# Graph layer with x in halves: the degrees of strips 3 to 9 taken in two steps of 256 rows

## The reference

```
A     = adj + I
deg   = sum(A, axis=1)
d     = rsqrt(deg)
h     = ((A * d[:, None]) * d[None, :]) @ x
y     = x + elu(h @ w)
out   = (y - mean(y)) / sqrt(var(y) + 1e-5)
```

## Time and profile before

| | |
|---|---|
| median of 3 runs | 1055.69 us (1055.21 to 1061.57) |
| profiled execution | 1055.05 us, its span 1053.3 us |
| PE, weight loads | 923.3 us, 831.4 us busy |
| DVE, ACT, POOL | 763.8, 703.6, 194.3 us busy |
| read from memory | 360.78 MB, 16 DMA engines nearly always busy until 1000 us |
| mean granted TensorE clock | 0.968 of full speed |

### The profile page before, as it was taken

How to read it: one execution, slowest core, us unless ns; L and a number is a source line. 1 busy time by engine, 2 the same in 40 slices (tenths; PEclk the granted TensorE clock), 3 DMA queues, 4 the chain that set the end, 5 groups by cost and what they waited for, 6 DMA issues and landing times. The chain is left out here.

```text
span 1053.3 us, 35548 instructions
## 1 busy us (share of the span) xinstructions
PE 923.3 (88%) x16000; PEld 831.4 (79%) x16000; DVE 763.8 (73%) x633; ACT 703.6 (67%) x1677; POOL 194.3 (18%) x267
## 2 busy tenths in 40 slices
PE   0089399399797998999999999999999999999995
PEld 0065288287797898899998997999999999999994
DVE  0496497576587667868788767997988797866933
ACT  6898798898888898898989989862214715031201
POOL 0120120210401304040412433466001101000000
PEclk9999689799899899999999999999999999999998
DMA  9999999999999999999999999989998898899920
GB/s 385 401 387 413 399 393 402 396 400 396 399 394 387 379 387 393 336 391 392 392 395 394 385 396 389 357 272 311 376 304 277 284 326 290 303 304 309 352 80 21
DMA packets 168809, 367.28 MB, mean 349 GB/s; under 512 B 6224, under 2 KB 32976, under 8 KB 158416
## 3 DMA queue, kind: packets, MB, share of 16 engines
q1 hardware_dynamic: 151616, 356.54, 91.4%
q10 hardware_dynamic: 17040, 8.46, 2.8%
HBM read 360.78 MB, written 4.19 MB: 347 GB/s over the span
## 5 line engine op out<-in xcount | busy, mean ns | idle before, releaser
L892 PE MATMUL p_set<-space 32*128 32x256 f32 (+3 forms) x15872 | 906.9, 386 | 117.6 <-ACT space L800 56.1
L892 PEld LDWEIGHTS p_set<-space 32*128 32x128 f32 x15872 | 816.0, 188 | 204.1 <-issue 132.3
L910 DVE STREAM_TRANSPOSE space<-space 128x2048 f32<-128x2048 f32 x256 | 579.5, 2292 | 113.6 <-ACT space L792 86.2
L792 ACT ACTIVATE space<-space 128x512 f32<-128x512 f32 (+2 forms) x744 | 578.8, 779 | 83.4 <-DMA space<-in_adj 76.4
L934 DVE TENSOR_TENSOR hT<-p_set,hT 128x1024 f32<-128x1024 f32 (+2 forms) x109 | 105.9, 991 | 118.6 <-PE p_set L892 118.6
L792 ACT ACTIVATION_READ_ACCUMULATOR space<-space 128x1 f32 x744 | 138.8, 187 | 0.0
L815 ACT ACTIVATE space<-space 128x512 f32<-128x512 f32 x16 | 10.1, 631 | 181.5 <-DVE space L945 181.3
L775 POOL COPY space<-xn 32x512 f32<-32x512 f32 x192 | 120.0, 625 | 12.3
L759 POOL TENSOR_TENSOR d<-deg,half 128x4 f32<-128x4 f32 x16 | 16.3, 1017 | 541.7 <-DVE deg L916 541.7
L800 ACT ACTIVATE space<-xn 32x512 f32<-32x512 f32 x96 | 60.2, 627 | 47.8 <-POOL xn L765 38.9
L782 POOL TENSOR_TENSOR rstd<-var_eps,half 128x4 f32<-128x4 f32 x16 | 16.5, 1031 | 239.0 <-DVE var_eps L979 239.0
(11 more groups left out here) (16 smaller groups left out, 28.8 us busy)
## 6 DMA issues: line engine op xcount, KB each, us to landing
space<-in_adj SPq DMA_DIRECT2D x332, 1024.0 KB, 12.2
xn<-in_x SPq DMA_DIRECT2D x20, 256.0 KB, 11.2
space<-in_x ACTq DMA_DIRECT2D x16, 256.0 KB, 7.2
out_rows<-space ACTq DMA_DIRECT2D x16, 256.0 KB, 7.1
space<-in_adj SPq DMA_DIRECT2D x4, 768.0 KB, 12.3
ident<-in_w ACTq DMA_DIRECT2D x1, 64.0 KB, 5.3
```

The source lines that it names most:

```text
L792: ins = nc.scalar.activation(view[:, g], view[:, g], ACT.Copy, accum_out=to[:, g:g + 1])
L892: ins = nc.tensor.matmul(to, xs_chunk(h, j)[quadrant(q)], moving, start=first and s == b == 0, stop=last and s == b == 3)
L910: nc.vector.transpose(slots[slot], slots[slot]).then_inc(tile_turned, 1)
```

## The change

For strips 3 to 9 the degrees are found in two halves of 256 rows (blocks 0 and 1, then 2 and 3). The upper rows of all near tiles land first, then x is asked for (behind the first of the lower pieces), then the lower rows follow in one go. Each half has its own row sum, power, scaling and its own 16 copies, half as long. When the upper half of x is in place, PE may open up to two jobs (`HALF_JOBS`) of two or more tiles of that band that are already turned, and multiply them with the upper half (b = 0, 1); each keeps its PSUM set until the lower half follows. A single near tile is now loaded by two DMAs of 512 KB instead of one of 1 MB.

With it go other constants: `KEPT` loses 57 - 56 = 1 tile in all (band 8 keeps one more, band 10 two fewer, band 12 two more, band 15 two fewer), so that 80 tiles instead of 79 are loaded again, and `FEED` falls from 14 to 10. Bands 0 to 7 keep what they kept. The near tiles of strips 3 to 9 become 4, 5, 4, 4, 3, 4 and 3. The number of tiles to multiply stays 256. POOL's constant `half` is renamed `minus_half`.

```diff
-KEPT = (1, 2, 3, 4, 5, 6, 5, 4, 4, 4, 5, 4, 1, 2, 3, 4)
+KEPT = (1, 2, 3, 4, 5, 6, 5, 4, 5, 4, 3, 4, 3, 2, 3, 2)
...
+HALVED = range(3, 10)
+HALF_JOBS = 2
+PIECES = 2
...
-FEED = 14
+FEED = 10
...
+def halves_of(r):
+
+    return tuple(range(PIECES)) if r in HALVED else (None,)
...
-    return items + sorted((("near", t, r) for t in range(r, BANDS) if (t, r) in kept), reverse=True)
+    near = sorted((("near", t, r) for t in range(r, BANDS) if (t, r) in kept), reverse=True)
+    if r not in HALVED:
+        return items + near
+    return items + near + [("split", r), ("rest", r)]
...
-            base, t0, nk = runs[0], left[w - 1][1], BLOCKS // w
+            base, t0 = runs[0], left[w - 1][1]
+            nk = BLOCKS // max(w, len(halves_of(r)))
             group = len(groups)
-            groups.append([w, list(range(len(tiles), len(tiles) + w))])
+            some = []
+            groups.append([BLOCKS // nk, list(range(len(tiles), len(tiles) + w)), some])
             for i in range(w):
                 row_todo.remove(("near", t0 + i, r))
                 take_slot(("tile", len(tiles)), base + i)
-                tiles.append(("first", t0 + i, r, base + i, [len(loads) + j for j in range(w)]))
-            return [("near", r, nk * j, nk, t0, w, base, j, group) for j in range(w)]
+                tiles.append(("first", t0 + i, r, base + i, some))
+            return first_piece([("near", r, nk * j, nk, t0, w, base, j, group) for j in range(BLOCKS // nk)])
         _, t, r = row_todo.pop(0)
-        return [tile_load("first", t, r)]
+        if r not in HALVED:
+            return [tile_load("first", t, r)]
+        slot, some, group = take_slot(("tile", len(tiles))), [], len(groups)
+        nk = BLOCKS // PIECES
+        groups.append([PIECES, [len(tiles)], some])
+        tiles.append(("first", t, r, slot, some))
+        return first_piece([("near", r, nk * j, nk, t, 1, slot, j, group) for j in range(PIECES)])
+
+    def first_piece(these):
+
+        if these[0][1] not in HALVED:
+            return these
+        many = BLOCKS // PIECES
+        rest.extend(v for v in these if v[2] >= many)
+        return [v for v in these if v[2] < many]
...
+        if row_todo and row_todo[0][0] == "split":
+            row_todo.pop(0)
+            pending_x.append(at_row)
+        if row_todo and row_todo[0][0] == "rest":
+            row_todo.pop(0)
+            queued.extend(sorted(rest, key=lambda v: v[2] // (BLOCKS // PIECES)))
+            rest.clear()
+            if queued:
+                return queued.pop(0)
+            end_row()
...
+        if at_row not in HALVED:
+            pending_x.append(at_row)
...
+    def row_summed(load):
+
+        r = load[3] if load[0] == "tile" else load[1]
+        k0, nk = (0, BLOCKS) if load[0] == "tile" else load[2:4]
+        for half in halves_of(r):
+            many = BLOCKS if half is None else BLOCKS // PIECES
+            base = many * half if half is not None else 0
+            rows = len(set(range(k0, k0 + nk)) & set(range(base, base + many)))
+            wide = 1 if load[0] == "tile" else load[5] if load[0] == "near" else load[5] // BAND
+            if rows:
+                sums_left[r, half] -= rows * wide
+                if not sums_left[r, half]:
+                    offer("dve", 0, "row_sum", (r, half), 0.35)
...
+                took = 0.14 + {"dve": 0.52, "act": 0.52, "pool": 0.58}[e] / len(halves_of_home(h))
+                offer(e, 0 if some is FIRST_COPIES else 4, "copies", (h, half, i), took * len(pairs))
...
+        for n, (job, home, these, piece) in enumerate(half_jobs):
+            if piece in usable[home]:
+                half_jobs[n] = (job, home, these, piece + 1)
+                if piece == PIECES - 1:
+                    half_jobs.pop(n)
+                parts.append((job, home, these, False, piece == PIECES - 1, piece))
+                return len(parts) - 1
...
+            for t in HALVED:
+                if len(half_jobs) >= HALF_JOBS or t not in home_of or 0 not in usable.get(home_of[t], ()) or whole(t):
+                    continue
+                some = [i for i in turned_early if tiles[i][:2] == ("first", t)]
+                these = next((c for m in range(min(MERGE, len(some)), 1, -1) for c in map(in_steps, combinations(some[:8], m)) if c), [])
+                if these:
+                    for i in these:
+                        turned_early.remove(i)
+                    rows = [tiles[i][2] for i in these]
+                    job = open_job(rows, {u: 1 for u in rows})
+                    half_jobs.append((job, home_of[t], these, 1))
+                    parts.append((job, home_of[t], these, True, False, 0))
+                    return len(parts) - 1
...
+        def xs_part(h, half, q, s):
+
+            return slots[homes[h][1]][quadrant(q), blocks_of(half), F * s:F * (s + 1)]
+
+        def x_part(h, half, s):
+            return xn[quadrant(s), h % XN, blocks_of(half)]
...
-                    r = arg
-                    pool.wait_ge(row_summed, row_nth[r])
-                    nc.gpsimd.tensor_tensor(d[:, r], deg[:, r % 2], half[:, :], ALU.pow).then_inc(d_ready, 1)
+                    r, half = arg
+                    blocks = blocks_of(half)
+                    pool.wait_ge(row_summed, row_nth[arg])
+                    nc.gpsimd.tensor_tensor(d[:, r, blocks], deg[:, r % 2, blocks], minus_half[:, blocks], ALU.pow).then_inc(d_ready, 1)
...
-                    h = arg
-                    t = homes[h][0]
-                    pool.wait_ge(d_ready, power_nth[t])
+                    h, half = arg
+                    t, blocks = homes[h][0], blocks_of(half)
+                    many = blocks.stop - blocks.start
+                    pool.wait_ge(d_ready, power_nth[t, half] if first_home(h) else known_nth(t))
                     pool.wait_ge(x_loaded[h % XN], 16 * (h // XN + 1))
-                    nc.gpsimd.tensor_tensor(xn[:, h % XN], xn[:, h % XN], d[:, t].unsqueeze(2).to_broadcast([128, BLOCKS, F]), ALU.mult)\
-                      .then_inc(x_scaled, 1)
+                    nc.gpsimd.tensor_tensor(xn[:, h % XN, blocks], xn[:, h % XN, blocks],
+                                            d[:, t, blocks].unsqueeze(2).to_broadcast([128, many, F]), ALU.mult).then_inc(x_scaled, 1)
                 elif kind == "copies":
-                    h, some = arg
...
+                    h, half, some = arg
+                    earlier = [k for k, _ in order["pool"][:order["pool"].index((kind, arg))]]
+                    pool.wait_ge(x_scaled, earlier.count("scale"))
+                    pool.wait_ge(d_ready, earlier.count("power"))
+                    if "diagonal" in earlier:
+                        pool.wait_ge(diagonal_added, earlier.count("diagonal"))
                     wait_vacant(pool, ("home", h))
                     for s, q in copies_of(h)[some][1]:
-                        nc.gpsimd.tensor_copy(xs_part(h, q, s), xn[quadrant(s), h % XN]).then_inc(copied_by["pool"], 1)
-                        pool.wait_ge(copied_by["pool"], copied[h, (s, q)][1])
+                        nc.gpsimd.tensor_copy(xs_part(h, half, q, s), x_part(h, half, s)).then_inc(copied_by["pool"], 1)
...
-                                               for e in {copied[h, (s, q)][0] for q in range(Q)}):
-                        pe.wait_ge(copied_by[engine], many)
-                    for b in range(BLOCKS):
+                    needed = [copied[h, v, (s, q)] for q in range(Q) for v in (halves_of_home(h) if half is None else (half,))]
+                    for engine in sorted({by for by, _ in needed}):
+                        pe.wait_ge(copied_by[engine], max(many for by, many in needed if by == engine))
+                    for b in range(BLOCKS)[blocks_of(half)]:
                         j = Q * b + s
...
-                            ins = nc.tensor.matmul(to, xs_chunk(h, j)[quadrant(q)], moving, start=first and s == b == 0, stop=last and s == b == 3)
+                            ins = nc.tensor.matmul(to, xs_chunk(h, j)[quadrant(q)], moving, start=first and s == 0 and b == blocks_of(half).start,
+                                                   stop=last and s == 3 and b == 3)
```

More of the change, by code:

```diff
@@ L85, in plan @@
     last_groups = row_groups(again)
-    sums_left = [len(strip_items(r, kept)) + r for r in range(BANDS)]
+    sums_left = {(r, half): (BLOCKS // len(halves_of(r))) * BANDS for r in range(BANDS) for half in halves_of(r)}
     first_left = [BANDS - sum(v[0] == t for v in again) for t in range(BANDS)]
@@ L120, in parts_left @@
     def parts_left():
-        return sum(len(p[2]) for p in parts) < BANDS * BANDS
+        return sum(len(p[2]) for p in parts if p[5] in (None, PIECES - 1)) < BANDS * BANDS
     def release(slot):
@@ L247, in issue @@
                     backlog += 1
-            elif load[0] == "near" and not load[7]:
-                coming.extend(groups[load[8]][1])
+            elif load[0] == "near":
```

(28 more changed lines are left out.)

150 lines of the change are left out of this document (85 added, 65 removed).

## The result

The changed kernel takes 1054.66 us (median of 22 runs, 1052.38 to 1057.09) against 1055.87 us (median of 22, 1054.46 to 1061.57). The ratio is 0.998, with a 95% interval of 0.9972 to 0.9988: faster by 0.2% (1.2 us between the medians), where 5.5 us or 0.5% was forecast. The profiled execution took 1054.86 us, its span is 1053.1 us; both kernels' traces are thus of about the same length (1053.3 us before), and single executions of one kernel lie up to 7 us apart.

The account below looks back on a forecast made before the run. PE was taken to be bound by gaps waiting for copies of x. The least of slack plus half-job gain over the strips, strip 7's 5.5 to 7.2, less 1, gave 5.5: 1055.05 to 1049.5 us, range 1041 to 1060.

Parts of the forecast that it names:

- What bounds it: PE's gaps wait for copies of x; the load queue sets when x_r is known; PE's gain by 597 us stays.
- rival C: Load queue, first phase: slots freed sooner bring degrees earlier by up to 3.5 us, so 1044 to 1046 us; chance 0.19.
- POOL's chain: POOL run twice at strips 3 to 9: 6.6 us a half, 13.2 instead of 10.5, costing nothing on the path.
- When the half job starts: PE begins the upper half at -2.9 us from the old power's start, or some 0.5 later behind an ACT sum.
- a late order: Deduction from strip 7's gain of 5.5 to 7.2 us: 1 us less for a late order and stalls.
- strip 5's 1.85 us of clock: PE behind the 4.6 us gap at strip 5 runs at 1.2 instead of 2.4 GHz; 1.85 us counted as gain.
- The sum up to band 10: Gain is the least over binding strips of slack plus half job; strip 7 least, 5.5 to 7.2 us, taken as 5.5.
- rival B: POOL's half copies cost nearly whole ones, lower x 3.2 us later, strips 7 and 9 gain 2.3 or nothing: 1053 to 1056; chance 0.20.
- Strip 10, not halved: Slack of 6.5 us before band 10 plus 3.5 us from tile (8, 4) in band 8 gives 10, so not binding.
- FEED and KEPT: Changed constants costed at 0, between -2 (slots free sooner) and +3 us (PE short of tiles within a strip).
- Rival D: Slots taken longer by (8, 4) and upper pieces leave 4 for transit, queue slower: 1055 + 0.5 to + 12, say 1061; chance 0.12.
- E (small loads): Up to 27 split tiles each pay 2.1 us more in turn, 57 us in all: 1106 us; chance 0.02.

Follow-up runs that it names:

- e1: Changed kernel, same plan, but PE's first half job of each band 3 to 9 waits for copies of both halves of x; 1095.34 us, ratio 1.036.
- e8: Changed kernel plus matmuls of constants in the gaps before the first half jobs of bands 3 to 5; 1057.72 us, 1.0007 against the kernel before.
- e4: Changed kernel with strip 10 halved too; 1052.86 us, 0.9967 against the kernel before.
- e5: Changed kernel with POOL's four copies of s = 3 given to ACT for bands 10 to 15; 1052.84 us, 0.996 against the kernel before.
- e9: Changed kernel with strip 10 halved too and POOL's four s = 3 copies given to ACT for bands 10 to 15; 1050.65 us, 0.9951 against the kernel before.
- e6: Kernel before, with POOL's four copies of s = 3 given to ACT for bands 10 to 15; 1056.86 us, ratio 1.001.
- e11: Changed kernel with FEED 14 as before; 1052.60 us, 0.9963 against the kernel before.
- e2: Changed kernel with no strip halved, so only KEPT and FEED differ from the kernel before; 1069.37 us, ratio 1.0116.
- e3: Halving of strips 3 to 9 alone, KEPT and FEED (14) as in the kernel before; 1061.73 us, ratio 1.0061.

## Why the prediction was wrong

The direction was right and the size was off: 5.5 us forecast, 1.2 us measured. Point by point:

**What bounds it.** Right: the gaps wait for copies of x, and PE's lead at 597 us is what is at stake. Wrong in one sentence: the time of x_r isn't the load queue's alone. e1 shows it coming later by the strip once PE is late. In the changed kernel SP waited less for PE (202 us instead of 238 between 55 and 560 us), yet rival C's bonus didn't come: the lower power of strip 5 ran no sooner than the whole strip's before, and of the dips in the transfers one moved to another place.

**POOL's chain.** The upper half of strip 5 and its lower half, in the changed kernel:

```profile
394.43 0.71 POOL L881 TENSOR_TENSOR d<-deg,minus_half 128x2 f32<-128x2 f32 x1 [45.46 <-DVE deg L1042]
395.21 0.61 POOL L888 TENSOR_TENSOR xn<-xn,d 128x256 f32<-128x256 f32 x1
395.89 5.43 POOL L899 COPY space<-xn 32x256 f32<-32x256 f32 x12
402.64 0.70 POOL L881 TENSOR_TENSOR d<-deg,minus_half 128x2 f32<-128x2 f32 x1 [1.32 <-DVE deg L1042]
```

One half takes 6.9 us against 6.6 forecast: a copy with its gap 5.43 / 12 = 0.45 (0.42), the power 0.71 (1.0: half the elements do save a third; the 0.10 us that it was argued from is a memset's), the scaling 0.7 (0.6). The lower power comes 0.8 us after that of the whole strip before. Strips 3 to 6 leave POOL idle between the halves; in strips 7 to 9 the lower power starts as the last upper copy ends, so there the margin was used up, as feared.

**When the half job starts.** The upper power came 7.4 us before the old one, 2.1 sooner than the 5.3 forecast. But the half job was to start 2.4 us behind it, and started 400.22 - 394.43 = 5.8 behind it. DVE's timeline of the changed kernel shows the rest:

```profile
395.80 1.23 DVE L1060 TENSOR_TENSOR hT<-p_set,hT 128x1024 f32<-128x1024 f32 x1 [1.46 <-PE p_set L1016]
396.94 2.30 DVE L1035 STREAM_TRANSPOSE space<-space 128x2048 f32<-128x2048 f32 x1
399.17 0.91 DVE L1049 COPY space<-xn 32x256 f32<-32x256 f32 x2
```

x was scaled at 395.82, and its two copies stood behind an add and a transpose for 3.3 us. The term "a late order" had 0.5 to 1 us for this. PE was idle 4.48 us meanwhile, and its clock was down: from 400 to 405 us it was granted half, 1.2 GHz. The forecast counted strip 5's 1.85 us of clock as won; they were not, and in e8, where they were, strip 7 took them back.

**The sum up to band 10.** Forecast 8.7 at strip 5, 7.3 at 6, 5.5 to 7.2 at 7, 7.6 at 8, in all 5.5. The lead that the account shows behind each strip is 4.4 us for 5 (129.8 - 125.4, the start of band 6), 4.8 for 6, 2.0 for 7 (129.8 - 127.8, the end of band 7) and 5.1 for 8. Each is 2.5 to 5 us less than I had for it, and the least is 2.0, not 5.5.

Strip 7 was the term that decided, and its half job, forecast at 3.5 us, gave nothing: the lead behind it is that strip's old slack of 2.0 us and no more. The lower half of x came later than the whole x had before. That is rival B, which priced this strip at a lead of 2.3 us. ACT's two copies of s = 0 ended at 511.79 instead of 509.94, and POOL held PE up once more:

```profile
510.94 0.85 ACT L924 ACTIVATE space<-xn 32x256 f32<-32x256 f32 x2
```

That the lead was 6.2 us at band 10 all the same is luck: it grew by waits of the kernel before that the forecast had not counted. At strip 8 PE was held up three times in one part, not once for 0.65 us, and once more in band 9:

```profile
558.40 2.01 PE L892 MATMUL p_set<-space 32*128 32x256 f32 x32 [0.65 <-POOL space L775]
561.09 34.94 PE L892 MATMUL p_set<-space 32*128 32x256 f32 x704 [0.68 <-POOL space L775]
596.82 13.50 PE L892 MATMUL p_set<-space 32*128 32x256 f32 x244 [0.79 <-POOL space L775]
```

In the account they cost 3.0 and 1.1 us, and the changed kernel has none of them. A lead is therefore not the least over the strips: behind the tightest one it can grow again.

**The step that failed.** Between band 10 and a 0 the lead falls from 6.2 to 0.7 us, and that is what lies between forecast and result. The step is the last one of the sum: "Strip 10, not halved: 6.5 + 3.5 = 10", and for KEPT "strips 11 and later had more slack than 10". From both it followed that nothing is lost behind strip 9. Band 9 of the kernel before began at 594.1, not 596.8 (that row is a wait inside its first part), so strip 10's slack was 4.8 us; 3.5 from (8, 4) against 6.2 won leave 2.1. At strip 11 the power ran at 648.69 before, so x was ready at 652.4 by the forecast's 3.7 us, and PE came at 664.2: slack 11.8. In the changed kernel PE comes 8.2 us sooner (a lead of 4.7 and one tile less ahead of it) and the power 2.2 us later: 1.4 are left. And slack was counted to the copies of s = 0 only. PE that comes just then is paced by POOL through s = 1 to 3: 1.4 us in each of bands 10 and 11. With 0.8 at 734 us it makes the fall to 2.2 us at a 10, with 1.3 at the first output that to 0.7 at a 0; the kernel before has none of these four waits. e4 and e5 each give 1.8 us back and e9 4.0, while e5's edit does nothing in the kernel before (e6). In e9 a lead of 4.9 us is left at a 0. The wait at the first output (1.06 us in e9) stays open.

POOL's lateness in these two strips has a second part that was not tried. The plan puts POOL's add of the diagonal between the scaling and the copies, here at strip 11 of the changed kernel:

```profile
652.98 1.27 POOL L874 TENSOR_TENSOR space<-space,ident 128x512 f32<-128x512 f32 x1
654.46 8.08 POOL L899 COPY space<-xn 32x512 f32<-32x512 f32 x12 [0.22 <-POOL space L874]
```

The copies end at 662.54 and PE goes on at 662.60. Behind the copies, as at strip 11 of the kernel before, the add would let them come 1.5 us sooner, and by these rows neither strip 10 nor strip 11 would hold PE up. That is an estimate.

**FEED and KEPT** "at 0, between -2 and +3": for FEED in the changed kernel the range holds (FEED 14 in its place is 2 us faster, e11), for KEPT and FEED together not. Without the halves they cost 13.6 us (e2), with them they save 7 (e3 against the changed kernel). They can't be priced apart from the rest. Rival D (slots, slower) did not come in the changed kernel; a lack of slots is what e3's waits point to. E (small loads) did not come: 30 loads of 512 KB land in 10.7 us where 1 MB takes 13.5, and the slices from 342 to 553 us carry 377 to 397 GB/s (336 to 395 before). The fixed cost and the half efficiency that the forecast takes from the Trainium skill (DMA: Bandwidth & Descriptors, Anatomy of one DMA) are given there for DMAs that GpSimd issues; these are issued by SP.

## What to carry to other kernels

In a chain of stages in which each waits for one that is fed from elsewhere, follow the lead through *all* stages to the end, also those the change doesn't touch: its worth is what the tightest of them lets through, and the waits of the old kernel behind that one, which are won as well. Here these hid that the tightest stage gave nothing. Count slack to the last input of a stage, not to its first, since an engine that arrives early is paced by the copies that arrive late. A queue with one buffer and in-order waits (the x load behind the copies) can stand for long and cost nothing (47.3 us in the kernel before), until everything around it is faster; look at it again then.

## What the hardware showed beyond this

POOL's power on 128x2 took 0.71 us where 128x4 takes 1.02: even with two or four elements in a row it goes by elements. From these two sizes I estimate 0.15 us for each and 0.4 fixed. POOL's copy of 32x256 took 398 ns against 623 for 32x512, ACT's 414 against 628: on these two, two half copies cost 0.17 to 0.2 us more than a whole one. DVE's times scatter too much for such a difference (237 to 477 ns for 32x256, mean 386).
